# Decoder layer: the first stage re-pipelined over four buffers, rope combination on GpSimd, context keys and values moved behind the first norm

## The chip, the cores and the metric

The kernel runs on one core of a Trainium2 chip. The metric is device time in microseconds, the median over runs of the whole program. "TensorE", "VectorE", "ScalarE" and "GpSimd" are the engines, called PE, DVE, ACT and POOL in the profile; SP is the sync engine, whose queue issues nearly all loads and stores here.

## What is computed

One decoder layer on 2048 tokens of width 256, with 16 heads of width 16: causal self attention with rope, cross attention, a mixture of eight experts, and a layer norm after each.

```python
x = layernorm(x + self_attention(x))      # q, k, v = x W + b; rope on q, k; softmax; Wo
qp = x @ Wq.T                             # cross attention
idx = argmax(qp @ ctx.T)                  # the nearest of 1601 context rows, for each token
mk, mv = split(ctx[idx] @ Wkv.T)          # one key and one value of width 16, shared by all heads
x = layernorm(x + (softmax(qh @ mk.T / 4) @ mv) @ Wc.T)
x = layernorm(x + experts(x))             # top 2 of 8, squared relu
```

Rope of a head's two halves: `x1*cos - x2*sin` and `x1*sin + x2*cos`. The key and the value of every context row (`ctx @ Wkv.T`) depend on no token, so they can be computed anywhere ahead of the cross attention.

## The kernel before

The program is a chain of blocks; a block ends when all engines are through, and the next one starts then. In a block each engine has its own list of instructions, which it runs in order, and the lists meet in semaphores. The first stage (lines 157 to 369) projects the tokens; then come the self attention (lines 421 to 711), the output projection with the first norm (`project_norm`, lines 714 to 837), the search of the nearest context row, the cross attention, and the experts.

**First stage.** Its work is 16 units (line 189): four chunks of 512 tokens, in each the queries and the keys (t = 0, 1), in each two halves m = 0, 1 of the 256 outputs. The halves of one projection are a *pair*, as rope needs both: x1 of all heads is in half 0 and x2 in half 1. A unit goes through all the engines:

- TensorE (lines 254 to 292): two float32 products of 512 columns into `pq` (two pair buffers), then two of 256 columns for the values of 128 tokens into `pv` (two buffers). From unit 5 on, the context keys: four column tiles of `ctx` (lines 276 to 283), and after unit 9 the context values, for each of 13 row tiles two products of 32 columns (lines 285 to 292), between two units.
- VectorE (lines 318 to 369): on the first unit of a pair four rope products from PSUM, `turned` and `crossed` (lines 331 to 339); in each unit the values with bias into `V` (line 342), the combination `whole` (line 348, subtract for m = 0, add for m = 1), and, once ScalarE has cast it, the remainder `rest` (line 353). The context adds the copies to `kvx` (line 361) and two subtractions of 16x1664 (lines 366 and 369).
- ScalarE (lines 295 to 315): the bf16 first part of `whole`, then the second part from `rest`; in between the copies and casts of the context keys.
- GpSimd (lines 232 to 250): memsets, the bf16 copies of the identity and the causal mask (lines 241 to 243, after a wait for their loads), then in each unit the third part, `rest` minus the second part (line 249).
- SP (lines 195 to 229): the loads, the identity and the mask last (lines 214, 215); then for each unit a store of its three parts to `qparts` or `kparts` in HBM (line 225), and ahead of the last unit's store the six loads of `kx` (line 223). At the end it waits for all of them.

`parts`, `rest` and `whole` have two buffers, so a unit's first part waits for the store of the unit two before it (line 312).

A float32 number is so sent as three bf16 parts; the attention multiplies six combinations of them (`PAIRS`, line 45) stacked on 96 partitions.

**Self attention.** SP loads the stacks from `qparts` and `kparts`: for the first group of heads per chunk, 12 loads of 16 partitions and 64 KB each, for the others per group (lines 676 to 686). Chunks 0 and 1 are loaded at the block's start (line 468), the load u + 2 after unit u's shift (line 477). GpSimd sets two rows of ones for each (lines 489 to 493). TensorE first zeroes its output bank with eight small products (line 527), then runs the score products of unit 0, of which VectorE takes the maxima (line 639); their shift goes back through SP into the stacks (line 476), and only then come the scores (line 560).

**First norm.** Per chunk TensorE turns the outputs of the attention (`turn`, 16 banks: n = 0 to 7 outputs, 8 to 15 normalised tokens), multiplies with `wo`, VectorE adds the residue and normalises, and the normalised tokens are turned back. ScalarE copies each bank (line 801), VectorE makes the remainder (`rest_of`, line 816). `pieces` are weights and context that are split into two float32r parts here: ScalarE makes the first (line 119), GpSimd the second (line 125), through `slots` buffers.

## Time and profile before

| | us |
|---|---|
| median of 3 runs | 1252.04 (1251.17 to 1254.86) |
| the profiled execution | 1248.05 |
| its span, from the first to the last instruction | 1246.3 |
| TensorE / VectorE / ScalarE / GpSimd busy | 1047.6 / 895.4 / 586.5 / 261.9 |
| first stage | 0 to 104.3 |
| self attention | 104.3 to 576.7 |
| output projection and first norm | 576.7 to 624.35 |
| mean granted TensorE clock | 0.908 of full |

Times in the rows are microseconds from the start of the span, unless marked ns. A row of a timeline has start, duration, engine, line and operation, the tiles written and read, the number of instructions merged, and in brackets the idle time before them with what ended it. A busy TensorE is not TensorE at its peak. Waits are inferred from semaphores. The first stage and the norm have no other stage's work beside them, because of the blocks.

### The profile page before, as it was taken

What the parts mean: (1) busy time and instruction counts of PE and PEld (TensorE: products, weight loads), DVE (VectorE), ACT (ScalarE), POOL (GpSimd) and SP (SyncE); (2) the same over time, 40 slices, a digit from 0 to 9 for tenths busy, and PEclk for the clock granted to TensorE, in tenths of its full rate; (3) what the DMA queues carried; (4) which work ended last, traced back from release to release, by engine and by line L of the source; (5) the groups of instructions that cost most, each with busy time, mean ns of one, the idle gap of its engine ahead of it and who ended that gap; (6) DMA issues with size and microseconds to landing.
All of it is one profiled execution on the core that took longest, in us unless ns stands there. A gap on an engine that the chain in (4) does not pass through costs nothing. (4 is left out here: it accounts for less than half of the span.)

```text
span 1246.3 us, 18037 instructions
## 1 busy us (share of the span) xinstructions
PE 1047.6 (84%) x6215; PEld 522.2 (42%) x6215; DVE 895.4 (72%) x1812; ACT 586.5 (47%) x804; POOL 261.9 (21%) x249
## 2 busy tenths in 40 slices
PE   6873999999999999997569976998989877879970
PEld 3441233333333333324458852232323315768860
DVE  3663899898789888712849988988888843755545
ACT  1320146666666666684234421665656552423322
POOL 2213010021112100003320005631011021332225
PEclk9885599999999999998879985999989987999995
DMA  7214127980000000004020003411111011142225
GB/s 247 102 50 90 49 36 82 109 82 1 1 2 2 1 1 2 1 2 142 0 73 33 27 1 104 139 60 44 44 32 55 14 36 44 61 144 70 72 72 175
DMA packets 60539, 71.70 MB, mean 58 GB/s; under 512 B 10333, under 2 KB 53725, under 8 KB 60445
## 3 DMA queue, kind: packets, MB, share of 16 engines
q1 hardware_dynamic: 54924, 59.04, 20.3%
q0 software_dynamic: 3408, 9.34, 2.1%
q10 hardware_dynamic: 2112, 2.10, 0.5%
q8 instruction: 55, 0.90, 0.3%
q14 instruction: 40, 0.32, 0.1%
HBM read 47.01 MB, written 22.85 MB: 56 GB/s over the span
## 5 line engine op out<-in xcount | busy, mean ns | idle before, releaser
L639 DVE TENSOR_REDUCE self_piece_max<-self_max 128x1 f32<-128x512 f32 (+3 forms) x640 | 349.4, 603 | 53.0 <-PE self_max L541 25.5
L606 ACT ACTIVATE self_probs<-self_scores 128x1024 f32<-128x1024 f32 (+3 forms) x320 | 274.1, 896 | 193.7 <-PE self_scores L560 192.7
L541 PE MATMUL self_max<-stack_k,stack_q 96*128 96x512 bf16 (+3 forms) x640 | 210.6, 368 | 12.2 <-DMA stack_k<-kparts 6.4
L1733 DVE TENSOR_REDUCE cross_piece_max<-banks 128x1 f32<-128x512 f32 x256 | 163.8, 682 | 26.5 <-PE banks L1624 24.8
L1701 ACT ACTIVATE cross_probs<-banks 128x1024 f32<-128x1024 f32 x128 | 126.5, 1022 | 106.1 <-PE banks L1647 104.0
L560 PE MATMUL self_scores<-stack_q,stack_k 98*128 98x512 bf16 (+3 forms) x640 | 170.6, 351 | 4.2 <-DMA stack_q<-self_shift 3.0
L571 PE MATMUL self_out<-self_probs,V 128*17 128x512 f32 (+3 forms) x1280 | 148.8, 537 | 2.6 <-ACT self_probs L606 2.0
L541 PEld LDWEIGHTS self_max<-stack_k,stack_q 96*128 96x128 bf16 x640 | 62.5, 98 | 179.6 <-DVE self_piece_max L639 130.7
L507 POOL TENSOR_SCALAR_AFFINE_SELECT self_probs<-self_probs 128x512 f32<-128x512 f32 x64 | 40.6, 635 | 398.5 <-ACT self_probs L606 398.2
L1624 PE MATMUL banks<-kx_few,stackx 97*128 97x512 bf16 x256 | 96.2, 416 | 23.2 <-DVE cross_piece_max L1733 14.5
L560 PEld LDWEIGHTS self_scores<-stack_q,stack_k 98*128 98x128 bf16 x640 | 57.2, 99 | 54.0 <-ACT self_probs L606 16.3
L1647 PE MATMUL banks<-stackx,kx_few 99*128 99x512 bf16 x256 | 78.8, 392 | 0.6 <-DMA stackx<-cross_shift 0.5
L1624 PEld LDWEIGHTS banks<-kx_few,stackx 97*128 97x128 bf16 x256 | 25.5, 100 | 113.9 <-DVE cross_piece_max L1733 67.3
L1656 PE MATMUL banks<-cross_probs,vx_few 128*17 128x512 f32 x512 | 70.1, 621 | 0.4 <-ACT cross_probs L1701 0.4
L1840 POOL DMA_INDIRECT ybuf<-ys,xin x39 | 37.7, 966 | 115.9 <-DVE ys L2021 114.8
L543 PE MATMUL self_max<-tri_b,ident_b 128*128 128x128 bf16 x256 | 59.2, 233 | 0.0
L1951 ACT CAST hT_first<-pt 128x512 fp32r<-128x512 f32 x39 | 22.9, 586 | 66.3 <-PE pt L1892 66.3
L101 PE MATMUL pp<-ctx_first,qp_first 128*128 128x512 f32 (+1 forms) x128 | 47.2, 369 | 3.2 <-DVE qp_rest L1068 2.0
L1263 POOL DMA_INDIRECT sent<-xd,expert_place x32 | 31.9, 996 | 84.8 <-DVE chosen_b L1399 70.2
L1045 ACT COPY near<-pp 128x512 f32<-128x512 f32 x64 | 30.7, 495 | 40.0 <-PE pp L101 39.9
L1995 DVE TENSOR_TENSOR square<-act_of 128x512 f32<-128x512 f32 x39 | 26.9, 691 | 28.9 <-ACT act_of L1944 28.9
L101 PE MATMUL pp<-ctx_rest,qp_first 128*128 128x512 f32 (+1 forms) x128 | 47.6, 372 | 0.0
(311 smaller groups left out, 1587.3 us busy)
## 6 DMA issues: line engine op xcount, KB each, us to landing
stack_q<-qparts SPq DMA_DIRECT2D x96, 64.0 KB, 8.3
stackx<-xparts SPq DMA_DIRECT2D x96, 64.0 KB, 2.3
xin<-sent SPq DMA_DIRECT2D x39, 129.0 KB, 2.0
stack_k<-kparts SPq DMA_DIRECT2D x18, 256.0 KB, 14.1
qparts<-parts SPq DMA_DIRECT2D x8, 384.0 KB, 2.5
kparts<-parts SPq DMA_DIRECT2D x8, 384.0 KB, 2.5
xparts<-xparts_sb SPq DMA_DIRECT2D x8, 384.0 KB, 2.8
o_tok<-in_w SPq DMA_DIRECT2D x4, 768.0 KB, 5.0
```

Of the source, the lines that this page charges most:

```text
L101: ins = nc.tensor.matmul(out, lhsT[a], rhs[b], start=first and n == 0, stop=last and n == len(terms) - 1)
L541: mm = nc.tensor.matmul(slot[:, 0:pc["w"]], pc["lhsT"], pc["rhs"], start=True, stop=not pc["diag"])
L543: mm = nc.tensor.matmul(slot[:, pc["w"] - P:pc["w"]], ident_b[:], tri_b[:], start=False, stop=True)
L560: mm = nc.tensor.matmul(ps[:, j, st["off"]:C], st["keys"](j), st["queries"](j), start=True, stop=True)
L571: mm = nc.tensor.matmul(po[32 * j:32 * j + VW, st["off"]:C], st["values"](j), probs[:, i % 3, j, st["off"]:C], start=st["first"], stop=st[ ...
L606: nc.scalar.activation(probs[:, i % 3, 2 * pair:2 * pair + 2, st["off"]:C], ps[:, 2 * pair:2 * pair + 2, st["off"]:C], ACT.Exp, scale=SCAL ...
L639: nc.vector.tensor_reduce(piece_max[:, u % 2, pc["row"], pc["at"]:pc["at"] + 1], slot[:, 0:pc["w"]], AX.X, ALU.max).then_inc(side_read, 1)
L1624: nc.tensor.matmul(slot[:, 0:pc["w"]], pc["lhsT"], pc["rhs"], start=True, stop=True).then_inc(side_ready, 1)
L1647: mm = nc.tensor.matmul(ps[:, j], st["keys"](j), st["queries"](j), start=True, stop=True)
L1656: mm = nc.tensor.matmul(po[32 * j:32 * j + VW], st["values"](j), probs[:, i % 3, j], start=st["first"], stop=st["last"], tile_position=(0, ...
L1701: nc.scalar.activation(probs[:, i % 3, 2 * pair:2 * pair + 2], ps[:, 2 * pair:2 * pair + 2], ACT.Exp, scale=SCALE).then_inc(probs_ready, 1)
L1733: nc.vector.tensor_reduce(piece_max[:, u % 2, pc["row"], pc["at"]:pc["at"] + 1], slot[:, 0:pc["w"]], AX.X, ALU.max).then_inc(side_read, 1)
```

## The change

**First stage.** `parts`, `rest`, `whole` and `pv` have four buffers instead of two. The engines go by pairs instead of units, each one pair deep behind the next: VectorE does the rope products of a pair, its two values, then the two remainders of the pair *before*; ScalarE the two first parts of a pair, then the two second parts of the pair before; GpSimd the two combinations `whole` of a pair (until now VectorE's), then the two third parts of the pair before. Context keys and values leave the stage, with their loads. The loads are reordered: the query weights and the first chunk first, the weights of values and keys behind the biases. GpSimd sets the ones of the first group's stacks here, ahead of its wait for identity and mask. `stack_q[0]` and `stack_k[0]` live through both stages, and SP issues the loads of chunk c - 1 in three groups of four, after the stores of units 1, 2, 3 of chunk c (c = 1 to 3), once all stores of chunk c - 1 have landed. The block ends when these have landed too; the attention loads only chunk 3 at its start.

**First norm.** The context keys and values are computed here as one product of 32 rows in split float32r, from the context that the norm splits anyway and a fourth piece, the split weights. TensorE does it ahead of the last two chunks' turns back and turns the values (13 transposes) ahead of the last. ScalarE copies four tiles and casts, GpSimd makes the two remainders (until now VectorE's), and SP loads `kx` at the end and waits for it.

The core of the diff:

```diff
+            stack_q = [sb(att, "stack_q0", [P, NC, GH, C], BF16)]
+            stack_k = [sb(att, "stack_k0", [P, GH, T], BF16)]
...
-                parts = sb(stage, "parts", [P, 2, 3, C], BF16)
-                rest = sb(stage, "rest", [P, 2, C])
+                parts = sb(stage, "parts", [P, 4, 3, C], BF16)
+                rest = sb(stage, "rest", [P, 4, C])
                 turned = sb(stage, "turned", [P, 2, 2, C])
                 crossed = sb(stage, "crossed", [P, 2, 2, C])
-                whole = sb(stage, "whole", [P, 2, C])
+                whole = sb(stage, "whole", [P, 4, C])
...
-                pv = psum(stage, "pv", [P, 2, C])
-                pk = psum(stage, "pk", [P, 2, C])
-                s_w, s_b, s_ctx = sem("weights_in"), sem("bias_in"), sem("ctx_in")
+                pv = psum(stage, "pv", [P, 4, C])
...
-                        for n, w in enumerate((wq, wk, wv)):
-                            sp.dma_start(w_sb[:, n], kt_view(w)).then_inc(s_w, 16)
+                        sp.dma_start(w_sb[:, 0], kt_view(wq)).then_inc(s_w, 16)
                         load_chunk(0, s_w, s_b)
                         for n, b in enumerate((bq, bk)):
                             sp.dma_start(bias[:, n], b).then_inc(s_b, 16)
+                        sp.dma_start(w_sb[:, 2], kt_view(wv)).then_inc(s_more, 16)
+                        sp.dma_start(w_sb[:, 1], kt_view(wk)).then_inc(s_more, 16)
                         sp.dma_start(bv_all[:], bv.rearrange("(a n) -> a n", a=1).to_broadcast([P, D])).then_inc(s_b, 16)
-                        load_chunk(1, s_x[1], s_x[1])
-                        sp.dma_start(ctx_sb[:], kt_view(ctxT)[:, :, 0:M]).then_inc(s_ctx, 16)
-                        sp.dma_start(wkv_sb[:], kt_view(xwkv)).then_inc(s_ctx, 16)
-                        for c in range(2, NC):
+                        for c in range(1, NC):
                             load_chunk(c, s_x[c], s_x[c])
                         sp.dma_start(ident[:], identity).then_inc(consts_in, 16)
                         sp.dma_start(tri[:], causal).then_inc(consts_in, 16)
                         for n, (t, m, c) in enumerate(units):
                             dst = (qparts, kparts)[t].rearrange("r (p m) t -> m p r t", m=KD)[m, :, :, c * C:(c + 1) * C]
-                            if n == len(units) - 1:
-                                sp.wait_ge(mk_split, 4)
-                                for i, (_, b) in enumerate(PAIRS):
-                                    sp.dma_start(kx[i * DK:(i + 1) * DK, :], mk_parts[:, b]).then_inc(s_mk_out, 16)
                             sp.wait_ge(p3_ready, n + 1)
-                            sp.dma_start(dst, parts[:, n % 2]).then_inc(s_parts_out[n % 2], 16)
-                        for i in range(2):
-                            sp.wait_ge(s_parts_out[i], 8 * len(units))
-                        sp.wait_ge(s_mk_out, 16 * len(PAIRS))
+                            sp.dma_start(dst, parts[:, n % 4]).then_inc(s_parts_out[n % 4], 16)
+                            if c and n % 4:
+                                if n % 4 == 1:
+                                    for i in range(4):
+                                        sp.wait_ge(s_parts_out[i], 16 * c)
+                                for to, there in stack_pairs(0, c - 1, c)[(n % 4 - 1) * 4:n % 4 * 4]:
+                                    sp.dma_start(to, there).then_inc(s_load[c - 1], 16)
+                        for i in range(4):
+                            sp.wait_ge(s_parts_out[i], 16 * NC)
                         sp.wait_ge(consts_in, 32)
+                        for c in range(NC - 1):
+                            sp.wait_ge(s_load[c], 16 * 2 * len(PAIRS))
                     @block.gpsimd
                     def _(pool):
...
                         pool.wait_ge(s_ones, 3)
                         nc.gpsimd.memset(kx[KS:KS + 3, :], 1.0).then_inc(s_ones, 1)
                         pool.wait_ge(s_ones, 4)
-                        nc.gpsimd.memset(mk[:], 0.0).then_inc(s_ones, 1)
-                        pool.wait_ge(s_ones, 5)
+                        for c in range(NC):
+                            if c:
+                                pool.wait_ge(s_set, c)
+                            nc.gpsimd.memset(stack_k[0][KS:KS + 2, :, c * C:(c + 1) * C], 1.0).then_inc(s_set, 1)
+                        pool.wait_ge(s_set, NC)
                         pool.wait_ge(consts_in, 32)
                         nc.gpsimd.tensor_copy(ident_b[:], ident[:]).then_inc(s_ones, 1)
                         nc.gpsimd.tensor_copy(tri_b[:], tri[:]).then_inc(s_ones, 1)
-                        for n in range(len(units)):
-                            pool.wait_ge(p2_ready, n + 1)
-                            if n:
-                                pool.wait_ge(p3_ready, n)
-                            nc.gpsimd.tensor_tensor(parts[:, n % 2, 2], rest[:, n % 2], parts[:, n % 2, 1], ALU.subtract).then_inc(p3_ready, 1)
-                        pool.wait_ge(s_ones, 7)
+                        for pair in range(len(units) // KD + 1):
+                            if pair < len(units) // KD:
+                                pool.wait_ge(qk_read, pair + 1)
+                                for m in range(KD):
+                                    n = KD * pair + m
+                                    if n >= 4:
+                                        pool.wait_ge(p1_ready, n - 3)
+                                        pool.wait_ge(rest_ready, n - 3)
+                                    half = (turned, crossed)[m]
+                                    nc.gpsimd.tensor_tensor(whole[:, n % 4], half[:, pair % 2, 0], half[:, pair % 2, 1],
+                                                            (ALU.subtract, ALU.add)[m]).then_inc(whole_ready, 1)
+                            if pair:
+                                for n in (KD * pair - 2, KD * pair - 1):
+                                    pool.wait_ge(p2_ready, n + 1)
+                                    nc.gpsimd.tensor_tensor(parts[:, n % 4, 2], rest[:, n % 4], parts[:, n % 4, 1], ALU.subtract).then_inc(p3_ready, 1)
+                        pool.wait_ge(s_ones, 6)
...
+                            if not n:
+                                pe.wait_ge(s_more, 16 * 2)
+                            if n >= 4:
+                                pe.wait_ge(v_read, n - 3)
                             for k in range(KD):
-                                last = nc.tensor.matmul(pv[:, n % 2, 0:D], xT_sb[:, k, n * P:(n + 1) * P], w_sb[:, 2, k, :],
+                                last = nc.tensor.matmul(pv[:, n % 4, 0:D], xT_sb[:, k, n * P:(n + 1) * P], w_sb[:, 2, k, :],
...
+                        for pair in range(len(units) // KD + 1):
+                            if pair < len(units) // KD:
+                                for n in (KD * pair, KD * pair + 1):
+                                    act.wait_ge(whole_ready, n + 1)
+                                    if n >= 4:
+                                        act.wait_ge(s_parts_out[n % 4], 16 * (n // 4))
+                                    nc.scalar.copy(parts[:, n % 4, 0], whole[:, n % 4]).then_inc(p1_ready, 1)
+                            if pair:
+                                for n in (KD * pair - 2, KD * pair - 1):
+                                    act.wait_ge(rest_ready, n + 1)
+                                    nc.scalar.copy(parts[:, n % 4, 1], rest[:, n % 4]).then_inc(p2_ready, 1)
...
+                                for n in (KD * pair, KD * pair + 1):
+                                    dve.wait_ge(v_ready, n + 1)
+                                    nc.vector.tensor_tensor(V[:, n, :, 0:DK], pv[:, n % 4, 0:D].rearrange("p (h d) -> p h d", h=H),
+                                                            bv_all[:].rearrange("p (h d) -> p h d", h=H), ALU.add).then_inc(v_read, 1)
+                            if pair:
+                                for n in (KD * pair - 2, KD * pair - 1):
+                                    dve.wait_ge(p1_ready, n + 1)
+                                    if n >= 4:
+                                        dve.wait_ge(p3_ready, n - 3)
+                                    nc.vector.tensor_tensor(rest[:, n % 4], whole[:, n % 4], parts[:, n % 4, 0], ALU.subtract).then_inc(rest_ready, 1)
...
-                        for n in range(2):
-                            load(n)
+                        load(NC - 1)
...
+                    sp.wait_ge(mk_split, 5)
+                    for i, (_, b) in enumerate(PAIRS):
+                        sp.dma_start(kx[i * DK:(i + 1) * DK, :], mk_parts[:, b]).then_inc(s_mk_out, 16)
+                    sp.wait_ge(s_mk_out, 16 * len(PAIRS))
...
+                    pool.wait_ge(mk_split, 2)
+                    nc.gpsimd.tensor_tensor(mk_rest[:], mk[0:DK, :], mk_parts[:, 0], ALU.subtract).then_inc(mk_split, 1)
+                    pool.wait_ge(mk_split, 4)
+                    nc.gpsimd.tensor_tensor(mk_parts[:, 2], mk_rest[:], mk_parts[:, 1], ALU.subtract).then_inc(mk_split, 1)
                 @block.tensor
                 def _(pe):
+                    def cross_keys():
+                        pe.wait_ge(split_done, len(pieces))
+                        for i, (a, b) in enumerate(mk_cols):
+                            if i >= 2:
+                                pe.wait_ge(mk_copied, i - 1)
+                            for k in range(KD):
+                                mm = product(pk[0:2 * DK, i % 2, 0:b - a], [w[:, k] for w in wkv_sb], [w[:, k, a:b] for w in ctx2], k == 0, k == KD - 1)
+                            mm.then_inc(mk_ready, 1)
+                    def cross_values():
+                        pe.wait_ge(mk_copied, len(mk_cols))
+                        pe.wait_ge(mk_split, 1)
+                        for t in range(MT):
+                            mm = nc.tensor.transpose(pk[:, 2, t * 2 * DK:(t + 1) * 2 * DK], mk[:, t * P:(t + 1) * P], ident[0:2 * DK, 0:2 * DK])
+                        mm.then_inc(mk_ready, 1)
                     def turn(n):
                         src, c, k = banks[n]
...
                             mm.then_inc(y_ready, 1)
                         if c >= 2:
                             turns(NC + c - 2)
+                    cross_keys()
                     turns(2 * NC - 2)
+                    cross_values()
                     turns(2 * NC - 1)
                 @block.scalar
...
                             first_of_piece(act, nc.scalar.copy, n - 3, pieces, raw, piece_in, first_done)
                         if k == KD - 1 and 2 <= n // KD < 2 + NC:
                             deviation(act, n // KD - 2, rstd, var_ready, std_ready)
+                        if n == KD * (2 * NC - 2) - 1:
+                            for i, (a, b) in enumerate(mk_cols):
+                                act.wait_ge(mk_ready, i + 1)
+                                nc.scalar.copy(mk[:, a:b], pk[0:2 * DK, i % 2, 0:b - a]).then_inc(mk_copied, 1)
+                            act.wait_ge(mk_copied, len(mk_cols))
+                            act.wait_ge(mk_split, 1)
+                            nc.scalar.copy(mk_parts[:, 0], mk[0:DK, :]).then_inc(mk_split, 1)
+                    act.wait_ge(mk_split, 3)
+                    nc.scalar.copy(mk_parts[:, 1], mk_rest[:]).then_inc(mk_split, 1)
                 @block.vector
                 def _(dve):
...
                         if c >= 2:
                             rest_of(c - 2)
                     normalise(dve, link, NC - 1, x_sb, mv, rstd, std_ready, normed)
-                    for c in range(NC - 2, NC):
-                        rest_of(c)
+                    rest_of(NC - 2)
+                    dve.wait_ge(mk_ready, len(mk_cols) + 1)
+                    for a, b, rows in ((0, M // P, P), (M // P, MT, M % P)):
+                        found = pk[0:rows, 2, a * 2 * DK:b * 2 * DK].rearrange("p (n d) -> p n d", d=2 * DK)
+                        nc.vector.tensor_copy(kvx[0:rows, a:b, 0:2 * DK], found)
+                        nc.vector.memset(kvx[0:rows, a:b, 2 * DK:DK + VW], 1.0)
+                    rest_of(NC - 1)
```

## Rows read from the trace of the kernel before

**Rows 1.** Window; busy PE, PEld, DVE, ACT, POOL; clock, DMA share, GB/s

```profile
60.00:70.00 10.00, 10.00 (x36) 7.43 (x36) 0.00 (x0) 0.00 (x0) 0.00 (x0) 0.59 0.00 0
```

**Rows 2.** Timeline of the first stage, TensorE and VectorE, around the context values

```profile
54.10 10.89 PE L290 MATMUL pk<-wkv_sb,ctx_sb 128*128 128x32 f32 x52 [5.07 <-ACT mk L303]
...
71.11 1.41 DVE L332 SCALAR_TENSOR_TENSOR turned<-pq,bias,cs 128x512 f32<-128x512 f32 x2 [15.33 <-PE pq L262]
```

**Rows 3.** The same timeline, VectorE, the first pairs

```profile
15.95 1.41 DVE L332 SCALAR_TENSOR_TENSOR turned<-pq,bias,cs 128x512 f32<-128x512 f32 x2 [15.95 <-PE pq L262]
...
23.21 1.41 DVE L332 SCALAR_TENSOR_TENSOR turned<-pq,bias,cs 128x512 f32<-128x512 f32 x2
...
25.84 0.41 DVE L342 TENSOR_TENSOR V<-pv,bv_all 128x256 f32<-128x256 f32 x1
```

**Rows 4.** The same timeline, TensorE, two units one after the other

```profile
13.94 1.88 PE L262 MATMUL pq<-xT_sb,w_sb 128*128 128x512 f32 x4
...
16.52 1.88 PE L262 MATMUL pq<-xT_sb,w_sb 128*128 128x512 f32 x4
```

**Rows 5.** Timeline, last store to first score product

```profile
101.05 0.58 SPq L225 DMA_DIRECT2D kparts<-parts  x1
...
104.31 2.05 PE L527 MATMUL self_out<-zeros 128*128 128x128 f32 x8 [16.70 <-PEq L193]
...
112.78 0.29 PE L541 MATMUL self_max<-stack_k,stack_q 96*128 96x128 bf16 x1 [6.42 <-DMA stack_k<-kparts]
```

**Rows 6.** Timeline of GpSimd, first stage; a window of 1 us

```profile
23.46 0.29 POOL L242 CAST ident_b<-ident 128x128 bf16<-128x128 f32 x1 [18.55 <-DMA tri<-in_causal]
...
20.00:21.00 1.00, 1.00 (x4) 0.50 (x4) 0.71 (x2) 0.25 (x1) 0.00 (x0) 1.00 1.06 389
```

**Rows 7.** One line (min/median/max ns); groups by form (busy us, mean ns)

```profile
L249 POOL TENSOR_TENSOR parts<-rest,parts x16: 1151/1158/2079, 24.0 to 99.4; 128x512 bf16<-128x512 f32 x16
...
L1597 POOL TENSOR_TENSOR w_rest<-o_tok,w_first 128x1024 fp32r<-128x1024 f32 x6 | 14.1, 2355 | 0.5
...
L313 ACT CAST parts<-whole 128x512 bf16<-128x512 f32 x16 | 9.9, 617 | 58.8 <-DVE whole L348 54.9 <-DMA qparts<-parts 3.9
...
L353 DVE TENSOR_TENSOR rest<-whole,parts 128x512 f32<-128x512 f32 x16 | 11.9, 746 | 11.8 <-ACT parts L313 11.8
```

**Rows 8.** Timelines of VectorE and GpSimd beside each other

```profile
84.21 1.87 DVE L366 TENSOR_TENSOR mk_rest<-mk,mk_parts 16x1664 f32<-16x1664 f32 x1
...
85.02 2.08 POOL L249 TENSOR_TENSOR parts<-rest,parts 128x512 bf16<-128x512 f32 x1 [4.50 <-ACT parts L315]
...
595.84 8.05 DVE L854 TENSOR_SCALAR x_sb<-x_sb,n_mv,n_rstd 128x256 f32<-128x256 f32 x4
...
597.66 6.09 POOL L125 TENSOR_TENSOR ctx_rest<-n_raw,ctx_first 128x1602 fp32r<-128x1602 f32 x2
```

**Rows 9.** DMA, 104 to 119 us: packets, MB; KB each, us to landing

```profile
q1 hardware_dynamic: 1920, 1.57, 66.7%
...
stack_q<-qparts SPq DMA_DIRECT2D x12, 64.0 KB, 3.4
```

**Rows 10.** Pace of split products; a cast of 16x1664; loads of kx; norm's end

```profile
1141.86 1.40 PE ph L101 x6
...
86.12 1.58 ACT L309 CAST mk_parts<-mk_rest 16x1664 bf16<-16x1664 f32 x1 [1.17 <-DVE mk_rest L366]
...
97.20 3.80 SPq L223 DMA_DIRECT2D kx<-mk_parts  x6
...
kx<-mk_parts SPq DMA_DIRECT2D x6, 52.0 KB, 2.3
...
624.35 0.21 POOL L938 MEMSET ones_b<- 128x128 bf16 x1 [20.60 <-POOLq L737]
```

**Rows 11.** Windows of 10 us in the self attention, columns of rows 1

```profile
130.00:140.00 10.00, 9.96 (x30) 2.50 (x28) 9.39 (x19) 1.02 (x1) 0.64 (x1) 0.50 0.00 1
...
160.00:170.00 10.00, 9.41 (x51) 3.01 (x49) 9.84 (x19) 4.47 (x5) 0.00 (x0) 1.00 0.00 0
```

146 lines of the change are left out of this document (36 added, 110 removed).

## Prediction, made before the changed kernel was run

> **What bounds the kernel now.** The table of 10 us stretches comes first, because the busy shares of the whole span say little about one stage. From 60 to 70 us TensorE is busy all the time at a granted clock of 0.59, while VectorE, ScalarE and GpSimd do nothing [rows 1]. The timeline names the work: the 26 small products of the context values start at 54.10 and hold TensorE for 10.9 us, the projections of the next pair queue behind them, and VectorE's first rope product of that pair comes at 71.11 after 15.33 us of idling [rows 2]. Elsewhere in the stage VectorE is the bound. A pair (the two units m = 0, 1 of one projection and chunk) starts on it at 15.95 and the next at 23.21, 7.3 us on [rows 3]; TensorE needs 2.58 us a unit, 5.2 a pair [rows 4]. The stage's last store is issued at 101.05, the attention's first instruction on TensorE starts at 104.31, and its first score product waits until 112.78 for the stacks, though TensorE was free at 106.4 [rows 5]. All this lies before the attention, with nothing beside it, so a microsecond saved here is one of the span.
>
> **First stage, start.** GpSimd makes the rope combinations (`whole`) in the new version, and they stand on its queue behind the wait for the identity and the mask, the last loads issued. Today that wait ends at 23.46 [rows 6] and hurts nobody, as GpSimd's first part is wanted about then. In the new order the context (1601 KB) and its weights (32 KB) are not loaded, 1.67 MB less at the 389 GB/s of that time [rows 6], 4.3 us: 19.2. Two casts of 0.3 us follow, so the first `whole` starts at 19.8. The four memsets of ones moved ahead of it (7.4 us together before) start near 3.4 and end by 11: covered by that wait. TensorE starts 2 to 3 us sooner, as one weight instead of three stands ahead of the first chunk; VectorE has its first pair near 13 instead of 15.95. GpSimd's wait covers this, and I book nothing for it.
>
> **First stage, pace.** VectorE loses two combinations a pair: four rope products take 2.63 us [rows 3], two values 0.33 each from issue to issue [rows 3], two `rest` about 0.6 each (0.69 to their ends, when alone; the mean of [rows 7] has waits in it): 4.5 a pair, under TensorE's 5.2. GpSimd gets four operations a pair. The third part takes it 1.16 us in the median, the 128x1024 subtraction 2.36 or 1.18 per 512 [rows 7]; so I take 1.17 for `whole`, 4.7 a pair. But these operations and VectorE's `rest` exclude each other. `mk_rest` on VectorE ran from 84.21 to 86.08 and the third part, issued at 85.02, took 2.08 instead of 1.16; four normalisations of 0.41 took 8.05 beside GpSimd's long subtractions, one let through after each [rows 8]. Rope products and values read one operand from PSUM and kept their length beside GpSimd. ScalarE's order adds a chain: both first parts of a pair come before both second parts of the pair before. A cycle is thus two `whole` (2.34), then a first and a second part on ScalarE (0.62 each [rows 7], with hand-over 1.35), then two third parts (2.34): 6.05 us. Two `rest` at 0.6 fall partly into ScalarE's 1.35 and partly between GpSimd's operations: 6.05 if all are hidden, 6.7 if one is not and arbitration alternates. I take 6.4. The Trainium skill (SBUF — State Buffer, Who interferes with whom) says that whichever of the two issues first keeps the shared ports for the whole instruction. By it alone, with no turn for VectorE between two queued operations, the cycle would be the 6.05 and the sum 2.1 us lower.
>
> From 19.8: two `whole` to 22.2, then `rest`, `whole`, `rest`, `whole` to 25.8, first part to 26.5, second to 27.1, two third parts to 29.5. That is unit 1; unit 13 is six cycles later, 67.9. Units 14 and 15 have no new `whole` between: 0.6 + 2.34 gives 70.9. Four buffers instead of two take away the wait for the store; they are not what paces it.
>
> **First stage, tail.** SP issues after each of units 13, 14, 15 one store and four stack loads: 3 x 0.36 + 12 x 0.47 from 67.9 is 74.6, and a load lands 3.4 us after its issue [rows 9], about 77.6. The block's end adds 0.7: the attention starts at 78.3 instead of 104.3, **26.0 us** less. A chunk is two cycles, 12.8 us; its 12 loads and 4 stores take 7.1 of them on SP, and the loads of the earlier chunks stay covered. If they delayed a store behind them by one load's 3.4 us, the four buffers would cover that too.
>
> **Attention.** The first chunk's stacks are there, so the first score product follows the zeroing products at once, as if at 106.4 instead of 112.78 [rows 5]: **6.4 us** less. Loading early costs 4.1 us at the tail (77.6 against a last store landing at 73.5), so of it 2.3 remain. From there on the order is unchanged. SP has 12 loads instead of 24 ahead of the first shift (free after 5.6 us, shift ready after some 11); nothing of chunk 3 is wanted before unit 3.
>
> **First norm.** Added here, per column tile: six products as in the pace of 1.40 us per six [rows 10], three tiles and a short one, 4.8 us after the last turned chunk of outputs at 615.6; so to 620.4, before the last two chunks of normalised tokens are turned. ScalarE's copies follow to 620.8, its cast of 16x1664 (1.58 [rows 10]) ends at 622.4. Then GpSimd subtracts 1664 columns. No row has this on GpSimd: 1602 columns took 3.05 [rows 8], 3.2 scaled; by the 2.36 for 1024 [rows 7] it is 3.8. I take 3.2, the row nearest in length. Cast 1.6 and a second subtraction 3.2 lead to 630.6. SP then issues the six loads of `kx`, 3.8 us, and they land 2.3 after [rows 10]: 636.7. The next block starts at about 637 instead of 624.35 [rows 10]: **12.7 us** more. The 13 turns of values, the copies to `kvx` (0.8) and the last `rest_of` end near 627, inside this chain. The weights piece waits for a free slot until the first subtraction ends (597.7), which holds ScalarE until about 600; VectorE is shut out by GpSimd until 603.8 then [rows 8], so it costs nothing. Bounds: a move fully covered would cost 0; with 3.8 each and late keys it is 16.
>
> **Sum.** -26.0 - 6.4 + 12.7 = -19.7. The profiled execution took 1248.05 us (span 1246.3), and it becomes 1228.4. The median of the three runs is 1252.04, 4.0 above it; the same difference taken from the median gives 1232.3. I say 1232.
>
> **Rivals.** A, the exclusion is lighter or the chain of ScalarE slips into it: TensorE's 5.2 a pair sets the pace. Six cycles 1.2 shorter save 7.2 us, and with a lighter end 9: 1223. For it: operations with a PSUM operand run free. Against: the 2.08 and 8.05. Chance 0.15.
> B, the first stage is slower: `whole` at 1.35 (the 128x512 subtraction in the norm, which had a wait in it), two `rest` never hidden, 7.3 a cycle, +5.4, and the norm at 16, +3.3: 1241. Chance 0.14. The same size comes from the stack loads, if they hold the stores up. The Trainium skill (SBUF — State Buffer, Door 1: The DMA port swizzle) speaks against such loads, since 16 partitions reach few ports: 104 GB/s measured there. The 24 loads here moved 1.57 MB in some 13.5 us, which is 116 GB/s, so the trace agrees [rows 9]. A chunk of loads is then 6.7 us, and its four stores of 0.39 MB at 389 GB/s are 4.0, together 10.7 of its 12.8: close, but covered.
> C, slower than before: TensorE's clock does not come back in the attention. It is at 0.50 from 130 to 140, where 30 products ran, against 51 in 10 us at full clock [rows 11], 4 us lost in ten. Before, it came back at 150, 26 us after the first scores. The stage begins here after another idle time (TensorE has nothing from about 58 to 78). If the clock stayed low for more than 50 us longer, the 19.7 are gone; at 60 us it is 1257. The equal program from the first scores on speaks against it. Chance 0.05.
> D, the change does not do what it says: the keys' tail in the norm and the identity's wait eat most of it, say the identity lands at 23.5 as now (+4.3), cycle 7.3 (+5.4), norm +6: 1248, no change. Chance 0.04. The forecast case has 0.62.
>
> **Numbers.** Its own case spans 1226 to 1238 (cycle 6.05 to 6.7, norm 11 to 15). With A and B the range is 1221 to 1243. A measurement of this kernel can tell about 0.3%, 3.8 us, from no change. Faster 0.91, same 0.04, slower 0.05.
>
> **What would show it.** In the first stage of the new profile: GpSimd's first `whole` near 19.8, waiting for the mask's load; `whole` starts 6.4 apart per pair; single `rest` or third parts of 1.2 to 2 us; no 15 us gap on VectorE. The attention's first instruction near 78 and its first score product 2.1 later. In the norm, SP's `kx` loads 15 us after the keys' last product, and SP's wait for them at the block's end. Wrong would be a first stage over 85 us or under 70, a norm more than 16 us longer, or a clock that returns at another distance from the first scores than 26 us.

## The result and the profile after the change

The changed kernel takes **1232.49 us** in the median of 4 runs (1230.31 to 1235.86), the kernel before 1251.61 us beside it (1250.03 to 1254.86, 4 runs): ratio 0.9846, 95% interval 0.9816 to 0.9876. On another chip, later, the same kernel took 1236.66 us (5 runs) against 1256.36 us (11 runs): 0.9833, 0.9808 to 0.9858. The profiled execution took 1232.33 us, its span is 1230.4 us.

The two spans by stage. The boundaries are the first rows of each stage in the timelines of SP and TensorE; the cross attention is counted from the issue of its second load of expert weights to VectorE's last product of a tile of its output.

| stretch | before | after | difference | forecast |
|---|---|---|---|---|
| start to attention's first instruction | 104.3 | 83.0 | -21.3 | -26.0 |
| self attention | 472.4 | 465.6 | -6.8 | -6.4 |
| first norm | 47.6 | 60.5 | +12.9 | +12.7 |
| nearest-row search and loads behind it | 152.6 | 149.3 | -3.3 | 0 |
| cross attention | 250.6 | 254.4 | +3.8 | 0 |
| rest | 218.7 | 217.5 | -1.2 | 0 |

The first stage first, in the chain of waits (engine, line, what it waited for: us in all, times, longest), from the start to 83 us:

```profile
engine line waited for: us in total, times, longest us
ACT parts L302 <- POOL whole L263: 29.5, 7, 18.5
DVE rest L338 <- ACT parts L302: 15.0, 10, 4.7
POOL parts L268 <- ACT parts L306: 14.8, 7, 3.7
DVE turned L321 <- PE pq L281: 14.0, 2, 12.3
ACT parts L302 <- DMA kparts<-parts: 12.9, 5, 3.7
ACT parts L302 <- DMA qparts<-parts: 8.5, 4, 3.4
```

VectorE's gap of 15.33 us [rows 2] is gone: of the 14.0 us that it waits for TensorE, 12.3 are the start. In its place ScalarE's first parts (L302) wait nine times, 21.4 us in all, for stores. The timeline of two pairs, ScalarE, GpSimd and SP's stores, shows what a store holds up:

```profile
46.48 2.28 POOL L268 TENSOR_TENSOR parts<-rest,parts 128x512 bf16<-128x512 f32 x2 [1.79 <-ACT parts L306]
47.66 0.38 SPq L224 DMA_DIRECT2D kparts<-parts  x1
48.71 1.27 POOL L263 TENSOR_TENSOR whole<-turned 128x512 f32<-128x512 f32 x1
...
50.17 0.43 SPq L224 DMA_DIRECT2D kparts<-parts  x1
50.52 0.62 ACT L302 CAST parts<-whole 128x512 bf16<-128x512 f32 x1 [3.60 <-DMA kparts<-parts]
...
53.64 0.62 ACT L302 CAST parts<-whole 128x512 bf16<-128x512 f32 x1 [2.50 <-DMA kparts<-parts]
54.16 1.13 ACT L306 CAST parts<-rest 128x512 bf16<-128x512 f32 x2
...
54.85 2.27 POOL L268 TENSOR_TENSOR parts<-rest,parts 128x512 bf16<-128x512 f32 x2 [3.65 <-ACT parts L306]
56.03 1.49 SPq L224 DMA_DIRECT2D qparts<-parts  x2
```

The third parts of a pair end at 48.7. The second of their stores is issued at 50.17 only, since four stack loads stand ahead of it on SP's queue, and ScalarE has its buffer back at 53.6. The first part that waits for it belongs to the pair after the next. But ScalarE's order puts it ahead of the second parts of the pair between, so these, and the third parts behind them, wait too: from one pair's third parts to the next, 46.48 to 54.85, it is 8.4 us. The step after that, in which the awaited stores had no loads between them, took 6.5 (61.37 in the same view). The last four third parts start at 69.78 and end at 74.26. The tail and the attention's start, SP and TensorE:

```profile
77.63 0.38 SPq L224 DMA_DIRECT2D kparts<-parts  x1
...
79.64 0.43 SPq L230 DMA_DIRECT2D stack_k<-kparts  x1
83.02 0.31 SPq L433 DMA_DIRECT2D stack_q<-qparts  x1
```
```profile
83.05 2.04 PE L489 MATMUL self_out<-zeros 128*128 128x128 f32 x8 [33.91 <-PEq L199]
84.88 0.31 PE L503 MATMUL self_max<-stack_k,stack_q 96*128 96x128 bf16 x1
```

The first score product comes 1.8 us after the attention's first instruction and waits for nothing; before it was 8.5 us [rows 5]. In the norm, the keys' chain (ScalarE, GpSimd, SP, then the next block):

```profile
592.49 0.20 PE L101 MATMUL pk<-ctx_first,xwkv_first 128*32 128x66 f32 x1
...
593.41 1.58 ACT L796 CAST mk_parts<-mk 16x1664 bf16<-16x1664 f32 x1
...
595.13 3.33 POOL L722 TENSOR_TENSOR mk_rest<-mk,mk_parts 16x1664 f32<-16x1664 f32 x1 [19.66 <-ACT mk_parts L796]
...
598.50 1.58 ACT L798 CAST mk_parts<-mk_rest 16x1664 bf16<-16x1664 f32 x1 [0.96 <-POOL mk_rest L722]
600.16 3.32 POOL L724 TENSOR_TENSOR mk_parts<-mk_rest,mk_parts 16x1664 bf16<-16x1664 f32 x1 [1.69 <-ACT mk_parts L798]
603.50 3.70 SPq L706 DMA_DIRECT2D kx<-mk_parts  x6
609.19 0.21 POOL L938 MEMSET ones_b<- 128x128 bf16 x1 [5.71 <-POOLq L694]
```

### The profile page after: what moved, and what is told of

It reads as the page before. It is cut to its first block and busy times, and to the rows that moved or that the text cites. A ratio compares the mean times of both kernels' runs of the same rounds, so it can differ in the third digit from the quotient of the medians.

```text
span 1230.4 us, 17963 instructions
## 1 busy us (share of the span) xinstructions
PE 1030.9 (84%) x6184; PEld 510.9 (42%) x6184; DVE 884.8 (72%) x1794; ACT 585.0 (48%) x805; POOL 286.3 (23%) x268
## 3 DMA queue, kind: packets, MB, share of 16 engines
q1 hardware_dynamic: 54652, 57.40, 19.8%
## 5 line engine op out<-in xcount | busy, mean ns | idle before, releaser
L1733 DVE TENSOR_REDUCE cross_piece_max<-banks 128x1 f32<-128x512 f32 x256 | 164.0, 683 | 27.9 <-PE banks L1624 25.9
```

Source lines behind the costliest of these rows:

```text
L1733: nc.vector.tensor_reduce(piece_max[:, u % 2, pc["row"], pc["at"]:pc["at"] + 1], slot[:, 0:pc["w"]], AX.X, ALU.max).then_inc(side_read, 1)
```

## The experiments

Theory 1: a loop over the store paces the first stage (third parts, store, first part of the pair after the next, second parts, third parts). Theory 2, the prediction's: GpSimd and VectorE exclude each other, and with ScalarE's order this paces it. Beside them: whether the early stack loads pay, what each part of the change is worth, and whether time gained ahead stays gained. All runs leave the computation whole. "Attention" below is TensorE's first instruction there (83.05 in the changed kernel), "first score" its first score product. A time without a number of runs is one execution; such times can't be ranked among each other, and the readings go by the stage boundaries. Those of the changed kernel's first stage repeat: in a second profile of it the attention starts at 82.89 and the last third parts at 69.62, against 83.05 and 69.78.

**`whole` back on VectorE.** The two combinations of a pair stand on VectorE ahead of its `rest`; all else as changed.

```diff
-                                    nc.gpsimd.tensor_tensor(whole[:, n % 4], half[:, pair % 2, 0], half[:, pair % 2, 1],
-                                                            (ALU.subtract, ALU.add)[m]).then_inc(whole_ready, 1)
...
+                                    nc.vector.tensor_tensor(whole[:, n % 4], half[:, pair % 2, 0], half[:, pair % 2, 1],
+                                                            (ALU.subtract, ALU.add)[m]).then_inc(whole_ready, 1)
```

> The combination whole goes back to VectorE, in the pipelined order by pairs, everything else as in the changed kernel. VectorE then has about 5.9 us a pair, GpSimd 2.3. Theory 1 (the loop over the store paces the stage): the pace stays at 6.5 to 8 us a pair, but the first combination comes at about 15 instead of 19.3, as it no longer stands behind the wait for the mask; the third parts still do. The attention starts at 79 to 83. Theory 2 (the exclusion paces it): with half of GpSimd's operations gone the pace is VectorE's 5.9 and the attention starts at 72 to 76. If moving the combination was worth much in itself, it starts later than 83.

1230.17 us. The first `whole` starts at 15.71 instead of 19.29, the attention at 82.49 instead of 83.05; ScalarE still waits 22.7 us for stores, and the third parts come 6.15 us apart early on. Theory 2 falls for this kernel: with half of GpSimd's operations gone the stage is as long, where theory 2 had 72 to 76. Nor was the move of `whole` to GpSimd worth anything here, with the early loads in place.

**Stack loads in the attention.** The 36 loads of chunks 0 to 2 leave SP's loop over the units and the attention issues them again.

```diff
-                                for to, there in stack_pairs(0, c - 1, c)[(n % 4 - 1) * 4:n % 4 * 4]:
-                                    sp.dma_start(to, there).then_inc(s_load[c - 1], 16)
...
-                        load(NC - 1)
+                        for n in range(2):
+                            load(n)
...
-                                if NC <= u + 2 < len(loads):
+                                if u + 2 < len(loads):
```

> The stacks of the first head group are loaded in the attention again, as in the kernel before; the first stage keeps its new pipeline. The prediction had the early loads worth 2.3 us net: 4.1 lost at the first stage's tail, 6.4 won at the attention's start. If the loads also hold up stores (theory 1b), the pairs lose the 8.4 us spacings and the stage ends 6 to 9 us sooner, at 74 to 77, and the first score product comes 8.5 us behind, at 83 to 86, against 84.9 now: the early loads would be worth about nothing. If they do not hold them up, the stage ends at 79 to 80 and the first score product comes at 87 to 89.

1230.94 us. SP, ScalarE and GpSimd at the end of the first stage, and TensorE in the attention:

```profile
60.56 1.26 POOL L255 TENSOR_TENSOR whole<-turned 128x512 f32<-128x512 f32 x1
...
64.49 4.48 POOL L260 TENSOR_TENSOR parts<-rest,parts 128x512 bf16<-128x512 f32 x4 [1.46 <-ACT parts L298]
...
72.68 2.04 PE L482 MATMUL self_out<-zeros 128*128 128x128 f32 x8 [23.19 <-PEq L199]
...
81.09 0.29 PE L496 MATMUL self_max<-stack_k,stack_q 96*128 96x128 bf16 x1 [6.36 <-DMA stack_k<-kparts]
```

The attention starts 10.4 us sooner than in the changed kernel and the first score product, in spite of its 6.4 us wait, 3.8 us sooner (81.09 against 84.88). Of the 10.4, 5.3 come before the last third parts (64.49 against 69.78), where no load holds a store up, and 5.1 at the tail. So the early loads win 6.6 us between the attention's start and the first score and cost 10.4 ahead of it: they lose 3.8.

**Casts behind the loop.** GpSimd's wait for identity and mask and the two casts move behind its loop over the pairs.

```diff
                         pool.wait_ge(s_set, NC)
-                        pool.wait_ge(consts_in, 32)
-                        nc.gpsimd.tensor_copy(ident_b[:], ident[:]).then_inc(s_ones, 1)
-                        nc.gpsimd.tensor_copy(tri_b[:], tri[:]).then_inc(s_ones, 1)
...
+                        pool.wait_ge(consts_in, 32)
+                        nc.gpsimd.tensor_copy(ident_b[:], ident[:]).then_inc(s_ones, 1)
+                        nc.gpsimd.tensor_copy(tri_b[:], tri[:]).then_inc(s_ones, 1)
                         pool.wait_ge(s_ones, 6)
```

> GpSimd casts identity and mask after its loop over the pairs instead of before it, so its first combination waits only for VectorE's rope products (about 15 us) and not for the mask (18.7). The prediction let the stage begin with this wait. If it is the gate, everything moves forward by 4 us and the attention starts at 79 (78.5 to 80). If the pace is set by the stores from the third pair on, counted from the first store, the same: the loop only starts earlier. If another start (the projections, 5.2 us a pair from 12.3 on) takes its place, it gains under 2 us: 81 to 83.

1233.91 us. The first `whole` starts 3.6 us sooner (15.74) and the attention 0.7 us sooner (82.32): the lead is lost again on the way, as ScalarE waits 25.0 us for stores instead of 21.4.

**Eight buffers**, with the stack loads as changed, and **eight buffers with the loads in the attention**:

```diff
-                parts = sb(stage, "parts", [P, 4, 3, C], BF16)
+                parts = sb(stage, "parts", [P, 8, 3, C], BF16)
```

> The changed kernel with eight buffers of parts instead of four; everything else, the stack loads in the first stage too, stays. In the changed kernel ScalarE's first parts wait 21 us in all for the stores of four units before. Theory 1 (that loop of store, first part, second part, third part is what paces the stage): ScalarE's waits for stores fall under 4 us, the pairs come 5 to 6 us apart all the way, the last group of third parts starts at 62 to 65 instead of 69.8 and the attention at 75 to 79 instead of 83.0. Rival 2 (the stack loads and stores on one queue pace the second half whatever the buffers): the waits for stores shrink, but SP's last loads stay at about 80 and the attention starts at 82 to 83. Rival 3 (my prediction's: the exclusion between GpSimd and VectorE and ScalarE's order pace it at 6.05 to 6.7 a pair): single third parts and `rest` lengthen to 1.5 us and over, the last group stays at 67.9 to 70.

> Eight buffers of parts, and the stack loads of the first group all in the attention (as in the run with loads in the attention and four buffers, where the pairs came 6.15 apart, the last third parts were stored from 67.9 and the attention started at 72.7). Nothing but stores is on SP's queue. Theory 1 (store loop): the waits for stores vanish, the pairs come at GpSimd's 4.7 to 5.2 us, the last stores are issued at 59 to 62 and the attention starts at 64 to 67. Rival 3 (exclusion and ScalarE's order, 6.05 to 6.7 a pair by my prediction): no change, last stores at 67 to 68, attention at 72 to 73. The first score product follows 8.4 us later in either case, as the stacks are loaded there.

1236.55 us and 1232.86 us (before, beside them: 1257.65). ScalarE no longer waits for a store in either. The attention starts at 76.75 with the early loads and at 71.81 without, the first score product comes at 78.59 and 80.07. The pairs are 5.98 us apart in both. One cycle of the second, VectorE, GpSimd and ScalarE:

```profile
47.92 1.27 POOL L257 TENSOR_TENSOR whole<-turned 128x512 f32<-128x512 f32 x1
...
49.87 1.92 DVE L332 TENSOR_TENSOR rest<-whole,parts 128x512 f32<-128x512 f32 x2 [0.76 <-ACT parts L296]
50.44 0.62 ACT L296 CAST parts<-whole 128x512 bf16<-128x512 f32 x1 [0.60 <-POOL whole L257]
50.97 1.13 ACT L300 CAST parts<-rest 128x512 bf16<-128x512 f32 x2
51.66 2.27 POOL L262 TENSOR_TENSOR parts<-rest,parts 128x512 bf16<-128x512 f32 x2 [1.25 <-ACT parts L300]
...
53.89 1.27 POOL L257 TENSOR_TENSOR whole<-turned 128x512 f32<-128x512 f32 x1
```

That is two `whole` (2.5), GpSimd's wait for ScalarE (1.25), two third parts (2.27): the prediction's cycle, close to its lower end of 6.05, with both `rest` hidden. Theory 1 holds for the loads (with them eight buffers are worth 6.3 us) and falls in its own size: without the loads four buffers cost 0.9 us only (72.68 against 71.81), and the 4.7 to 5.2 us a pair and the start at 64 to 67 that it expected are not reached, since ScalarE's order is next. With eight buffers the early loads pay 1.5 us at the first score.

**Second parts first.** Four buffers and the early loads as changed; ScalarE's two blocks alone change places.

```diff
+                            if pair:
+                                for n in (KD * pair - 2, KD * pair - 1):
+                                    act.wait_ge(rest_ready, n + 1)
+                                    nc.scalar.copy(parts[:, n % 4, 1], rest[:, n % 4]).then_inc(p2_ready, 1)
                             if pair < len(units) // KD:
...
-                            if pair:
-                                for n in (KD * pair - 2, KD * pair - 1):
-                                    act.wait_ge(rest_ready, n + 1)
-                                    nc.scalar.copy(parts[:, n % 4, 1], rest[:, n % 4]).then_inc(p2_ready, 1)
```

> The changed kernel, four buffers, with ScalarE's order alone turned round: the second parts of the pair before stand ahead of the first parts of a pair. A first part that waits for a store then holds up no second part. Theory 1 (the loop runs over ScalarE's order): third parts no longer come behind the store of the pair before; the last group starts at 63 to 67 instead of 69.8, the attention at 77 to 80. Rival 2 (SP's queue with the stack loads paces the second half): 82 to 83 as now. Rival 3 (GpSimd and VectorE exclude each other): 81 to 83, with longer single operations.

> The kernel with ScalarE's second parts first once more, timed in rounds and with a second profile. Its attention started 10.9 us earlier than the changed kernel's and the block behind the norm 12.2 us earlier, yet its execution was 0.9 us shorter only, as the cross attention took 263.7 us instead of 254.4 and the expert stage 74.5 instead of 72.1. Theory 4 (the giving back belongs to the kernel's timing): again 262 us or more, median 1229 to 1232. Rival (chance of one execution): 250 to 256 in the new profile, median 1220 to 1223.

1231.57 us in one execution; later, on another chip, 1231.79 us (6 runs) against 1254.9 (11 runs), ratio 0.9804, 0.9766 to 0.9841. The attention starts at 72.14 in the first profile and at 76.16 in the second, of one and the same program. The first stage has two rhythms. First the first profile, then the second, a cycle each, GpSimd and VectorE's `rest`:

```profile
32.55 2.37 DVE L338 TENSOR_TENSOR rest<-whole,parts 128x512 f32<-128x512 f32 x2
32.65 1.71 POOL L263 TENSOR_TENSOR whole<-turned 128x512 f32<-128x512 f32 x1
...
34.33 1.73 POOL L263 TENSOR_TENSOR whole<-crossed 128x512 f32<-128x512 f32 x1
...
36.01 2.28 POOL L268 TENSOR_TENSOR parts<-rest,parts 128x512 bf16<-128x512 f32 x2
...
38.24 1.73 POOL L263 TENSOR_TENSOR whole<-turned 128x512 f32<-128x512 f32 x1
```
```profile
34.43 1.27 POOL L263 TENSOR_TENSOR whole<-turned 128x512 f32<-128x512 f32 x1 [0.58 <-DVE crossed L325]
34.93 3.00 DVE L338 TENSOR_TENSOR rest<-whole,parts 128x512 f32<-128x512 f32 x2
35.66 1.72 POOL L263 TENSOR_TENSOR whole<-crossed 128x512 f32<-128x512 f32 x1
...
37.34 2.72 POOL L268 TENSOR_TENSOR parts<-rest,parts 128x512 bf16<-128x512 f32 x2
...
40.64 1.26 POOL L263 TENSOR_TENSOR whole<-turned 128x512 f32<-128x512 f32 x1 [0.58 <-DVE crossed L325]
```

In the first GpSimd is never idle and a pair takes 5.59 us. In the second `rest` is issued a little later against GpSimd's operations, waits longer (3.00 for the two), the rope products behind it are late, GpSimd waits 0.58 for them, and a pair takes 6.21. The first `whole` starts at 19.01 and 19.55 in the two. That is not what tells the rhythms apart: the two kernels further down that have this order too both go at 6.21 us a pair, one with its first `whole` at 19.05. VectorE's first rope product comes at 12.23 in the profile with 5.59, and at 12.72, 13.75 and 14.32 in those with 6.21. With the loop over the store gone, GpSimd's operations, of which some show 1.72 us instead of 1.27, fill the whole pair in the first rhythm and all but 0.58 us of it in the second. That theory 2's exclusion paces the stage here is read from these rows; no run took it away.

The second profile's cross attention (the stage's length is taken up below) took 260.0 us, under theory 4's 262 and over the rival's 256; the median was in theory 4's range. Of the 6.9 us gained at the attention's start the ratios show little (0.9804 against 0.9833 and 0.9846 for the changed kernel), but their intervals overlap widely, so these runs alone can't say.

**Keys earlier in the norm.** The keys' products stand ahead of the outputs of the third chunk, ScalarE's copies and casts at the matching places.

```diff
                         pe.wait_ge(t_read, (c + 1) * KD)
+                        if c == NC - 2:
+                            cross_keys()
...
-                    cross_keys()
                     turns(2 * NC - 2)
...
-                        if n == KD * (2 * NC - 2) - 1:
+                        if n == KD * NC - 1:
```

> The changed kernel with the first norm's order changed: the products of the context keys stand ahead of the products of the third chunk of outputs (TensorE waits there for 10.6 us), ScalarE's copies and first cast behind the last copy of output tiles, its second cast behind the first chunk of normalised tokens. The values' transposes stay. Theory: the norm's end is the chain copies, cast 1.6, subtraction 3.3, cast 1.6, subtraction 3.3, loads 3.7 + 2 behind the keys' last product; with the keys' end at about 580 instead of 592.9 this chain ends by 599, and the norm ends with the last chunk of tokens, 3 to 4 us later than it would without the keys in the way: 60.5 us becomes 53 to 56. Rival (GpSimd's two subtractions of 3.3 us shut VectorE out while it has the statistics and normalisation of chunks 2 and 3 to do, so the chunks come later by as much): 57 to 60.

1230.72 us. The norm takes 55.0 us instead of 60.5, inside the 53 to 56 of the theory. In the two kernels further down that have this order too it takes 57.8 and 54.7. The keys' first product runs at 574.84, in a wait that TensorE had anyway, and SP's loads of `kx` are over before the last tokens are turned (TensorE, SP, next block):

```profile
574.84 0.60 PE L101 MATMUL pk<-ctx_first,xwkv_first 128*32 128x512 f32 x1 [10.56 <-POOL xwkv_rest L125]
...
592.07 3.70 SPq L706 DMA_DIRECT2D kx<-mk_parts  x6
...
601.95 0.21 POOL L940 MEMSET ones_b<- 128x128 bf16 x1 [9.90 <-POOLq L694]
```

**The keys moved, nothing else.** The first stage of the kernel before (two buffers, `whole` on VectorE, no early loads) without context, keys and values; the norm of the changed kernel.

```diff
-                            if 0 <= i < len(mk_cols):
-                                a, b = mk_cols[i]
-                                if i >= 2:
-                                    pe.wait_ge(mk_copied, i - 1)
...
+                    cross_keys()
                     turns(2 * NC - 2)
```

> One part of the change alone: the context keys and values are moved into the first norm as in the changed kernel; the first stage is that of the kernel before (two buffers, `whole` on VectorE, no stack loads), without the context. Before, the keys cost the first stage a stall of 15.3 us on VectorE and some 4.6 us of VectorE's own work. Theory 1 (the changed stage is held by its store loop and gains little from its pipelining): this kernel's attention starts at 84 to 86, that is all but 1 to 3 us of the 21.3 us that the changed kernel's first stage gained come from the moved keys, and the pipelining with four buffers is worth nearly nothing. Rival (the pipelining carries its share): the attention starts at 88 or later. In either case the first score product follows 8.4 us after the attention's start, and the norm takes 60 to 61 us.

1247.33 us. TensorE in the attention:

```profile
80.54 2.04 PE L455 MATMUL self_out<-zeros 128*128 128x128 f32 x8 [13.04 <-PEq L183]
...
89.14 0.29 PE L469 MATMUL self_max<-stack_k,stack_q 96*128 96x128 bf16 x1 [6.56 <-DMA stack_k<-kparts]
```

The attention starts at **80.54**, sooner than in the changed kernel and sooner than either theory had it, after pairs 7.44 us apart; the norm takes 60.0. The block behind the norm starts at 612.77 instead of 624.35: of the 15.2 us that the changed kernel has gained there (609.19), this move alone has 11.6. At the first score product, where the parts can be summed (from there to the norm every one of these profiles takes 462.9 to 463.9 us):

| first stage | first score product | step |
|---|---|---|
| before | 112.78 | |
| keys and values moved out | 89.14 | -23.6 |
| and pairs over four buffers, `whole` on GpSimd | 81.09 | -8.0 |
| and the early stack loads: the changed kernel | 84.88 | +3.8 |
| and ScalarE's second parts first, two profiles | 73.97, 78.00 | -10.9, -6.9 |

The 8.0 us of the pipelining were not parted further into buffers, order by pairs and order of the loads.

**All three orders, and does it stay gained?** Second parts first, keys earlier, casts behind the loop. The block behind the norm started up to 12 us earlier in the runs above, yet single executions were hardly shorter. A theory 4 was formed for it: what is gained ahead is given back by TensorE's clock in the cross attention.

> The changed kernel with three orders changed: ScalarE's second parts ahead of its first parts (attention started at 72.1 instead of 83.0 alone), the keys' products ahead of the third chunk's outputs in the norm (55.0 us instead of 60.5 alone), the casts of identity and mask behind GpSimd's loop (0.7 us). If the parts add up, the attention starts at 71 to 72, and the block behind the norm at 591 to 592 instead of 609.2. Theory 4 (time gained ahead of the nearest-row search and the cross attention is given back there, as TensorE's clock is granted less in them): the cross attention, 254.4 us from its first load to its last tile in the changed kernel and 263.7 in the run with the second parts first, takes 262 us or more, and the whole is 1223 to 1230. Rival (no giving back, the longer stages were chance): the cross attention takes 250 to 256 and the whole is 1214 to 1217.

1226.87 us (6 runs) against 1254.9: ratio 0.9768, 0.9729 to 0.9807. The attention starts at 74.30 and not at 71 to 72 (the slower rhythm), the block behind the norm at 597.51 and not at 591 to 592 (the norm takes 57.8 here, with more of its products at 0.63 instead of 0.40 us), the cross attention takes 261.8. The whole is inside the range of theory 4 and the cross attention just under its 262, so the changed kernel was run once more beside the kernel before, with a mended version that leaves the casts where they were:

> The changed kernel once more, beside the next one and the kernel before on the same chip, timed in rounds and with a second profile. It is the yardstick for the mended order, whose rounds were on another chip. Its first stage should repeat: the attention starts at 82 to 84, the block behind the norm at 608 to 610. Open is how much of the later stages is chance: its cross attention took 254.4 us, those of seven kernels that start it earlier 253.8 to 263.7, that of the kernel with the old first stage 262.6. If the long ones belong to an earlier start, this one takes 252 to 256 again (theory 4); if they are chance of the execution, it may as well take 258 to 264, and its ratio to the kernel before stays at 0.982 to 0.988.

> The changed kernel with ScalarE's second parts first and the keys' products ahead of the third chunk's outputs; the casts of identity and mask stay where the change has them. Alone the first was worth 10.9 us at the attention's start in one profile and 6.9 in the next (pairs 5.59 and 6.21 us apart), the second 5.6 us in the norm. If both hold, the block behind the norm starts at 591 to 596 instead of 609.2, 13 to 18 us earlier. By theory 4 (the later stages give time back through the clock) the median is then 5 to 9 us under that of the changed kernel beside it; by the rival (what is gained stays) it is 13 to 18 us under it.

The changed kernel again: 1236.66 us (1232.39 to 1242.06, 5 runs), the attention at 82.89, the block behind the norm at 607.90. The mended one: **1223.68 us** (1217.82 to 1227.24, 6 runs), ratio to the kernel before 0.9734, 0.9706 to 0.9762, against 0.9833 for the changed one beside it: 13.0 us less, at the lower end of what the rival expected; the two intervals lie apart. Its attention starts at 76.04, in the slower rhythm, the block behind its norm at 595.05, 12.9 us sooner than in the profile beside it. And the changed kernel's cross attention, 254.4 us in its first profile, took **264.3** in this one, though it started at the same time (758.49 and 758.2 us). The windows of 20 us of the first profile and of the second (columns of rows 1):

```profile
758.00:778.00 20.00, 19.26 (x100) 5.87 (x98) 18.56 (x34) 12.86 (x14) 12.06 (x6) 0.95 0.49 163
...
958.00:978.00 20.00, 15.37 (x86) 5.29 (x87) 16.79 (x53) 11.15 (x15) 0.62 (x1) 1.00 0.06 17
```
```profile
758.00:778.00 20.00, 19.77 (x94) 5.88 (x93) 17.58 (x31) 11.98 (x13) 11.06 (x6) 0.84 0.50 161
...
958.00:978.00 20.00, 17.07 (x85) 7.70 (x85) 15.74 (x36) 8.27 (x10) 1.04 (x1) 0.91 0.08 21
```

Theory 4 falls: the length of this stage varies between executions of one program. In the profiles here it lies between 250.6 (the kernel before) and 264.3 us, most of them above 257. The granted clock roughly goes with it: over its first 250 us it is 0.96 of full in the shortest and 0.92 in the five of 261.8 and more, but 0.95 in one of 253.9 and one of 258.9 alike. What is gained ahead of it stays gained.

## Why the prediction came out right

**The bound.** Right. VectorE's gap at the context values was the stage's largest loss; taken out alone, with the keys' own work, it gave 23.6 of the 27.9 us at the first score product, and 11.6 of 15.2 behind the norm that takes the work over.

**Start.** Right in its numbers, wrong in its weight. The first `whole` came at 19.29 (19.8 foretold) behind the wait for the mask, TensorE at 6.10, VectorE at 12.28. But this wait was taken as the gate of the stage, and moved away it gave 0.7 us.

**Pace.** Too fast by more than its range allowed. The price of `whole` was 1.27 us in the profile (1.17 foretold). From the first third parts (26.39) to those of unit 12 (69.78) the changed kernel has six pairs in 43.4 us, 7.2 each, and 6.4 were foretold (6.05 to 6.7). The cycle was right for another kernel: it is 6.15 where no load holds a store up and 5.98 where nothing waits for stores. The Trainium skill (SBUF — State Buffer, Who interferes with whom) says that the one that starts first holds the shared pair for the whole instruction and the other blocks. For single operations the rows agree (2.08 us for 1.16 [rows 8]), but between two queued operations of GpSimd one `rest` was let through: `whole` then shows 1.72 instead of 1.27 us. The order that the two engines fall into goes with 5.59 or 6.21 us a pair.

**The step that failed** is the sentence "If they delayed a store behind them by one load's 3.4 us, the four buffers would cover that too", and with it "Four buffers instead of two take away the wait for the store". Four buffers are two pairs; ScalarE's order, which the prediction named for another reason, takes one of them away, since a first part that waits for a store stands ahead of the second parts of the pair before. Twice a store delayed by loads then made the third parts 2.2 us later, and with smaller delays it was 5.3 us before the last third parts, against the kernel with the loads in the attention. With nothing but stores on the queue the second of the two sentences nearly holds: there four buffers cost 0.9 us. Unit 13's third part was foretold for 67.9; the last four start at 69.78, so it ended near 72.0. The tail was 11 us from there (foretold 10.4). The attention started at 83.0 instead of 78.3; 4.1 of these 4.7 us were there at unit 13's third part already. The early loads, foretold to win 2.3 us net, lost 3.8.

**Attention.** -6.8 for -6.4. The clock came back as foretold, 26 us after the first scores (95.98); the windows of the changed kernel around it (columns of rows 1):

```profile
114.00:122.00 8.00, 7.54 (x30) 2.41 (x29) 6.02 (x14) 1.83 (x3) 0.63 (x1) 0.51 0.01 1
122.00:132.00 10.00, 8.96 (x64) 3.24 (x61) 9.96 (x21) 4.38 (x7) 3.07 (x3) 1.00 0.00 0
```

The granted clock is at its lower level (1.2 GHz, 0.50 to 0.52 of full in the windows) from 94 to 122 us and full (2.4 GHz) from there. Rival C is out.

**Norm.** +12.9 for +12.7, each step in its place: keys' end 44.2 us after the norm's start (43.7), subtractions 3.33 and 3.32 (3.2), loads of `kx` 3.70 (3.8), landed and closed at 609.19. The loads were issued 10.8 us behind the keys' last product; the prediction's own steps give 10.2, and the 15 in its list of signs does not fit them. Part of the price was avoidable: 5.5 of the 12.9 us go when the keys are put into TensorE's 10.6 us wait.

**The sum.** The three terms give -15.2 instead of -19.7, and the medians differ by 19.1 and, on the other chip, 19.7. Other stages lie between. The nearest-row search took 3.3 us less, which the prediction did not have: GpSimd's wait for a load at its start fell from 2.66 to 0.93 us, and its first long window had a granted clock of 1.00 instead of 0.93. This gain repeats: the search took 149.0 to 150.7 us in all thirteen profiles whose norm computes the keys, also in the one with the old first stage, and 152.6 in the profile before. The rest's -1.2 is within its spread over all the profiles (216.6 to 220.2), and the cross attention's +3.8 within what it varies between two executions of one program. So the shown terms give some -18.5, and that the medians came to -19.1 and -19.7 is in part luck: the number was met, 1232.49 for 1232, with the first stage 4.7 us too hopeful and a term left out that is nearly as large. The mechanism of rival B's second form (loads that hold the stores up) is what happened, with 4.7 us of its 8.7; of A only the light exclusion was seen, in another order.

**Left open.** Why the search's clock was higher behind the longer norm. What sets which of the two rhythms the stage takes. Whether with second parts first the early loads pay was not tried. Why a cross attention is granted less clock in one execution than in the next.

## What to carry over

Count a ring of buffers in pairs of the loop that uses it, and then look at the order of the engine that waits for a free one: what stands behind the wait in its queue, and belongs to older work, shrinks the ring. Small loads put into a store's queue cost what they delay; price them at the store's consumer, and not on the queue's total. And measure one part alone before crediting the whole: here the plain removal of one stall was most of the gain (11.6 of 15.2 us behind the norm), and a change of two orders, with no new resource, was worth 13 us more.

## What the hardware did that was not expected

- One program has two steady rhythms in a stage where GpSimd and VectorE share operands in SBUF: 5.59 and 6.21 us a pair, 4.0 us at the attention's start. Of four profiles with this order one had the faster one, that in which VectorE's first rope product came earliest (12.23 against 12.72 to 14.32); whether this sets it is not shown.
- The cross attention of one and the same program took 254.4 and 264.3 us in two profiles, more than half of what the change is worth. A single profiled execution of each kernel can't tell a gain of 10 us made ahead of it; the stage boundaries ahead of it can.
- A store of 384 KB landed 2.6 us after its issue in the median where only stores were on the queue (eight buffers, loads in the attention); behind four loads of 64 KB ScalarE had its buffer 3.5 us after the issue (50.17 to 53.64), and the issue itself was 1.4 us late. The Trainium skill (SBUF — State Buffer, Door 1: The DMA port swizzle) has such loads, of 16 partitions, at a low rate; the direct price here was not their bytes but the stores behind them.
